# Causal filter and step sizes of a state-space block: half of the filter on TensorE, a shorter series, a comparison on GpSimd, one function table

## The reference, cut to what matters

```
x = lax.conv_general_dilated(x, conv1d_w, (1,), [(DC - 1, 0)], dimension_numbers=('NCH', 'OIH', 'NCH'), feature_group_count=DI)
x = silu(x + conv1d_b[None, :, None])
x_dbl = jnp.einsum('ed,bdl->bel', x_proj_w, x)
dt_lo = x_dbl[:, :DTR]
Bm = x_dbl[:, DTR:DTR + DS]
Cm = x_dbl[:, DTR + DS:]
delta = jnp.einsum('dr,brl->bdl', dt_proj_w, dt_lo)
delta = jax.nn.softplus(delta + dt_proj_b[None, :, None])
...
dBu = jnp.einsum('bdl,bnl,bdl->lbdn', delta, Bm, x)
```

## Time and profile before

| | us |
|---|---|
| median of 3 runs (7186.41 to 7193.9) | 7189.62 |
| the profiled execution, its own time | 7190.81 |
| its span, first to last instruction | 7189.0 |
| block of `filter_and_steps`, first image | 5901.4 to 6027.3 |
| the same, second image | 6417.6 to 6544.0 |

### The profile page before, as it was taken

How to read it: one execution, slowest core, us unless ns; L and a number is a source line. 1 busy time by engine, 2 the same in 40 slices (tenths; PEclk the granted TensorE clock), 3 DMA queues, 4 the chain that set the end, 5 groups by cost and what they waited for, 6 DMA issues and landing times. The chain is left out here.

```text
span 7189.0 us, 96561 instructions
## 1 busy us (share of the span) xinstructions
PE 5186.9 (72%) x22687; PEld 3143.4 (44%) x22687; DVE 5423.3 (75%) x10561; ACT 4492.4 (62%) x11845; POOL 4824.1 (67%) x4571
## 2 busy tenths in 40 slices
PE   7777676776766666666676766676889966757768
PEld 6444444444444344443444443332544434645644
DVE  5777777777777777777777777773769988988972
ACT  4666666666666666666666666775337758958940
POOL 3777777777777777777777777772029965945920
PEclk9999999999999999999999999887999987987989
DMA  7887887878878788787887878886000011231234
GB/s 220 285 250 239 248 250 236 251 238 248 250 237 250 239 248 251 236 251 239 248 251 236 251 238 246 293 284 203 28 21 33 33 49 49 103 110 60 103 122 165
DMA packets 584384, 1400.46 MB, mean 195 GB/s; under 512 B 94035, under 2 KB 258144, under 8 KB 579424
## 3 DMA queue, kind: packets, MB, share of 16 engines
q0 software_dynamic: 308224, 1006.95, 46.3%
q1 hardware_dynamic: 273506, 385.08, 15.8%
q10 hardware_dynamic: 2304, 4.20, 0.2%
HBM read 1314.13 MB, written 81.67 MB: 194 GB/s over the span
## 5 line engine op out<-in xcount | busy, mean ns | idle before, releaser
L627 POOL DMA_INDIRECT st_corners<-corner_table,df_rows x3840 | 3637.9, 947 | 1266.4 <-issue 1048.9
L1000 ACT ACTIVATE st_corners<-st_corners,df_share 128x128 f32<-128x128 f32 x3840 | 1225.7, 390 | 1555.4 <-DMA st_corners<-corner_table,df_rows 1516.0
L900 PE MATMUL df_acc_ps<-df_turned,df_tapw 128*128 128x512 f32 x3840 | 2006.9, 649 | 38.8 <-DMA df_tapw<-in_tap_w_dram 35.4
L889 PE MATMUL df_turn_ps<-main_ident,df_sampled 128*128 128x128 f32 x3840 | 646.6, 295 | 1426.7 <-DVE df_sampled L673 1369.7
L889 PEld LDWEIGHTS df_turn_ps<-main_ident,df_sampled 128*128 128x128 f32 x3840 | 445.5, 148 | 2208.3 <-issue 2096.0
L668 DVE TENSOR_TENSOR st_corners<-st_corners,df_part_ps 128x512 f32<-128x512 f32 x960 | 660.3, 688 | 850.6 <-ACT df_part_ps L1000 838.2
L1000 ACT ACTIVATE df_part_ps<-st_corners,df_share 128x128 f32<-128x128 f32 x3840 | 1178.8, 351 | 35.2 <-DVE df_sampled L673 34.6
L173 PE MATMUL st_conv_ps<-st_ow,st_patch 128*128 128x147 f32 (+1 forms) x6272 | 994.0, 306 | 1.1 <-issue 1.1
L900 PEld LDWEIGHTS df_acc_ps<-df_turned,df_tapw 128*128 128x128 f32 x3840 | 737.5, 210 | 579.5 <-issue 538.7
L173 PEld LDWEIGHTS st_conv_ps<-st_ow,st_patch 128*128 128x128 f32 x6272 | 895.8, 201 | 9.6 <-issue 9.0
L657 DVE TENSOR_TENSOR st_corners<-st_corners,df_weight_ps 128x512 f32<-128x512 f32 x960 | 657.3, 685 | 275.0 <-DMA st_corners<-corner_table,df_rows 270.1
(11 more groups left out here) (373 smaller groups left out, 5613.9 us busy)
## 6 DMA issues: line engine op xcount, KB each, us to landing
df_tapw<-in_tap_w_dram SPq DMA_DIRECT2D x962, 128.0 KB
sc_c_row<-c SPq DMA_DIRECT2D x128, 512.0 KB, 3.6
st_corners<-corner_table,df_rows POOLq DMA_INDIRECT x3840
y_b<-st_outs SPq DMA_DIRECT2D x128, 256.0 KB, 5.2
l1f_w<-in_w_dram SPq DMA_DIRECT2D x32, 1024.0 KB, 6.9
fu_spare<-y_b SPq DMA_DIRECT2D x64, 256.0 KB, 5.4
f_y_in<-y_b SPq DMA_DIRECT2D x64, 256.0 KB, 5.7
u<-dw_u SPq DMA_DIRECT2D x64, 256.0 KB, 2.1
```

The costliest lines, as they stand in the source:

```text
L627: nc.gpsimd.indirect_dma_start(corners[slot][:, j].rearrange("p v c -> p (v c)"), None, tables[g // GPB], bass.IndirectOffsetOnAxis(ap=row ...
L889: t = nc.tensor.transpose(turn_ps[pair][:, j * TILE:(j + 1) * TILE], sampled[pair][:, j, :], ident[:])
L900: m = nc.tensor.matmul(acc_ps[:, h, :], tapw[pair][:, h * P:(h + 1) * P], turned_sb[pair][:], start=first, stop=last, skip_group_check=not ...
L1000: nc.scalar.activation(dst, src, ACT.Copy, scale=share[slot][:, j - VT, v:v + 1]).then_inc(weighed_a, 1)
```

## The change

- Three quarters of the filter of half 0 (chunks 0 to 5, six of the eight) go to TensorE: four products with diagonal weight matrices `diag` per chunk, into PSUM tiles that lie idle at that time. ScalarE builds the four diagonals. VectorE keeps five of the eight units of 1024 columns (`TAPPED`), one after the other and no longer two interleaved.
- The silus follow the new order: silu(0), silu(1), keep_low(0), keep_low(1), soften(0), silu(2), silu(3), soften(1). The loop over c keeps its order on ScalarE, TensorE and VectorE.
- The series runs in a unit in which its leading coefficient is one, so that it needs four operations on each half and not five. The exponential makes e in that unit through its bias, and the logarithm takes it back through its scale.
- The comparison (`large`) moves from VectorE to GpSimd, `bound(c)`. GpSimd runs bound(0), and then for each c: bound(c+1), du(c).
- Two explicit loads name one table that has both exp and log.

```diff
-    SERIES = (1.0 / 5, -1.0 / 4, 1.0 / 3, -1.0 / 2, 1.0)
-    LIMIT = 2.0 ** -5
+    UNIT = 0.2 ** 0.2
+    SERIES = [c / UNIT ** n for n, c in ((4, -1.0 / 4), (3, 1.0 / 3), (2, -1.0 / 2), (1, 1.0))]
+    LIMIT = UNIT * 2.0 ** -5
+    CONVOLVED = (PARTS - 1) * LP // SPAN
+    TAPPED = [(1, 0), (1, 1), (0, PARTS - 1), (1, 2), (1, PARTS - 1)]
...
+        def conv_ps(c):
+            if c in (2, 3):
+                return delta_ps[c - 2][:]
+            return dut_ps[c % 2][:].rearrange("p j d -> p (j d)")
...
+            def convolve(c):
+                pe.wait_ge(u_loaded[c * SPAN // LP], 16 * HALVES)
+                if c >= 4:
+                    pe.wait_ge(active, active_by_pe(c - 4))
+                for k in range(CONV1):
+                    m = nc.tensor.matmul(conv_ps(c), diag[:, k, :], u[0][:, c * SPAN + k:c * SPAN + k + SPAN],
+                                         start=(k == 0), stop=(k == CONV1 - 1))
+                m.then_inc(filtered, 1)
...
+            pe.wait_ge(cleared, HALVES)
+            pe.wait_ge(diagonals, CONV1)
+            for c in range(4):
+                convolve(c)
             project(0)
             widen(0)
             project(1)
+            for c in range(4, CONVOLVED):
+                convolve(c)
+            pe.wait_ge(active, ACTIVE[PARTS - 1])
...
+            for k in range(CONV1):
+                nc.scalar.activation(diag[:, k, :], ident[:], ACT.Copy,
+                                     scale=conv1_sb[:, 0, b, k:k + 1]).then_inc(diagonals, 1)
...
-                    nc.scalar.activation(e_sb[s][h][:], e_sb[s][h][:], ACT.Exp, scale=-1.0).then_inc(exped, 1)
+                    nc.scalar.activation(e_sb[s][h][:], e_sb[s][h][:], ACT.Exp, scale=-1.0,
+                                         bias=log_unit[:]).then_inc(exped, 1)
...
             silu(0)
+            silu(1)
+            nc.scalar.preload_act_table_set("natural_log_exp_and_others")
             keep_low(0)
+            keep_low(1)
             soften(0)
-            keep_low(1)
+            silu(2)
+            silu(3)
+            nc.scalar.preload_act_table_set("natural_log_exp_and_others")
             soften(1)
-            for q in range(1, PARTS):
-                silu(q)
...
+                    if k == 0:
+                        ins = v.tensor_scalar(dst, src, w, None, ALU.mult)
+                    else:
+                        dve.wait_ge(tapped, n * CONV1 + k)
...
-                    own.done(v.tensor_scalar(poly[h][:], e_sb[s][h][:], SERIES[0], SERIES[1], ALU.mult, ALU.add))
-                for term in (0.0, *SERIES[2:]):
+                    own.done(v.scalar_tensor_tensor(out=poly[h][:], in0=e_sb[s][h][:], scalar=SERIES[0],
+                                                    in1=e_sb[s][h][:], op0=ALU.add, op1=ALU.mult))
+                for term in SERIES[1:]:
...
-                for h in both:
-                    v.tensor_scalar(large[h][:], e_sb[s][h][:], LIMIT, None, ALU.is_ge).then_inc(bounded, 1)
...
+            def bound(c):
+                for h in range(HALVES):
+                    pool.wait_ge(exped, HALVES * c + h + 1)
+                    if c >= 1:
+                        pool.wait_ge(stepped, HALVES * (c - 1) + h + 1)
+                    nc.gpsimd.tensor_scalar(large[h][:], e_sb[c % 2][h][:], LIMIT, None, ALU.is_ge).then_inc(bounded, 1)
+
+            bound(0)
             for c in range(GPB):
+                if c + 1 < GPB:
+                    bound(c + 1)
```

More of the change, by code:

```diff
@@ L1 @@
+import math
 from contextlib import ExitStack
@@ L2187, in filter_and_steps @@
         du = [sb(f"du{s}", [P, HALVES, SPAN]) for s in range(2)]
+        diag = sb("diag", [P, CONV1, P])
+        log_unit = sb("log_unit", [P, 1])
         low_ps = pb("low_ps", [P, SPAN])
@@ L2193, in filter_and_steps @@
         cleared = sem("cleared")
+        diagonals = sem("diagonals")
+        filtered = sem("filtered")
         tapped = sem("tapped")
@@ L2214, in cols, with active_by_pe @@
             return slice(c * SPAN, (c + 1) * SPAN)
+        def conv_ps(c):
+            if c in (2, 3):
+                return delta_ps[c - 2][:]
+            return dut_ps[c % 2][:].rearrange("p j d -> p (j d)")
+        ACTIVE = []
+        for q in range(PARTS):
+            ACTIVE.append((ACTIVE[-1] if ACTIVE else 0) + (2 + 1 if q < PARTS - 1 else HALVES))
+        def active_by_pe(c):
+            return c // 2 * 3 + c % 2 + 1
         @block.sync
@@ L2283, in _ @@
         def _(act):
+            for k in range(CONV1):
+                nc.scalar.activation(diag[:, k, :], ident[:], ACT.Copy,
+                                     scale=conv1_sb[:, 0, b, k:k + 1]).then_inc(diagonals, 1)
             act.wait_ge(loaded, 16 * 4)
-            act.wait_ge(one_set, 1)
+            act.wait_ge(one_set, 2)
             def silu(q):
-                for h in range(HALVES):
-                    act.wait_ge(tapped, (q + 1) * CONV1 * HALVES - HALVES + h + 1)
+                if q < PARTS - 1:
+                    for c in range(q * LP // SPAN, (q + 1) * LP // SPAN):
+                        act.wait_ge(filtered, c + 1)
+                        nc.scalar.activation(xs_sb[:, 0, cols(c)], conv_ps(c), ACT.Silu,
+                                             bias=conv_b[:, 0:1]).then_inc(active, 1)
+                for h in (1,) if q < PARTS - 1 else range(HALVES):
+                    act.wait_ge(tapped, CONV1 * (TAPPED.index((h, q)) + 1))
                     part = xs_sb[:, h, q * LP:(q + 1) * LP]
@@ L2312, in soften @@
                     act.wait_ge(valued, 4 * c + 2 * h + 2)
-                    nc.scalar.activation(e_sb[s][h][:], e_sb[s][h][:], ACT.Exp, scale=-1.0).then_inc(exped, 1)
+                    nc.scalar.activation(e_sb[s][h][:], e_sb[s][h][:], ACT.Exp, scale=-1.0,
+                                         bias=log_unit[:]).then_inc(exped, 1)
                 for h in range(HALVES):
                     act.wait_ge(exped, HALVES * c + h + 1)
-                    nc.scalar.activation(ln_sb[s][h][:], e_sb[s][h][:], ACT.Ln, bias=one[:]).then_inc(logged, 1)
+                    nc.scalar.activation(ln_sb[s][h][:], e_sb[s][h][:], ACT.Ln, bias=one[:],
+                                         scale=1.0 / UNIT).then_inc(logged, 1)
             def keep_turned(c):
@@ L2345, in _ @@
             v.memset(one[:], 1.0).then_inc(one_set, 1)
+            v.memset(log_unit[:], math.log(UNIT)).then_inc(one_set, 1)
             for h in both:
@@ L2348, in _, with taps @@
             dve.wait_ge(cleared, HALVES)
-            n = 0
-            for q in range(PARTS):
+            def taps(n):
+                h, q = TAPPED[n]
                 dve.wait_ge(u_loaded[q], 16 * HALVES)
                 for k in range(CONV1):
-                    for h in both:
-                        src = u[h][:, q * LP + k:q * LP + k + LP]
-                        dst = xs_sb[:, h, q * LP:(q + 1) * LP]
-                        w = conv1_sb[:, h, b, k:k + 1]
-                        if k == 0:
-                            ins = v.tensor_scalar(dst, src, w, None, ALU.mult)
-                        else:
-                            dve.wait_ge(tapped, n - HALVES + 1)
-                            ins = v.scalar_tensor_tensor(out=dst, in0=src, scalar=w, in1=dst, op0=ALU.mult, op1=ALU.add)
-                        ins.then_inc(tapped, 1)
-                        n += 1
+                    src = u[h][:, q * LP + k:q * LP + k + LP]
+                    dst = xs_sb[:, h, q * LP:(q + 1) * LP]
+                    w = conv1_sb[:, h, b, k:k + 1]
+                    if k == 0:
+                        ins = v.tensor_scalar(dst, src, w, None, ALU.mult)
+                    else:
+                        dve.wait_ge(tapped, n * CONV1 + k)
+                        ins = v.scalar_tensor_tensor(out=dst, in0=src, scalar=w, in1=dst, op0=ALU.mult, op1=ALU.add)
+                    ins.then_inc(tapped, 1)
+            for n in range(len(TAPPED)):
+                taps(n)
             for c in range(GPB):
```

3 lines of the change are left out of this document (2 added, 1 removed).

## The result

| | before | after |
|---|---|---|
| median, us | 7188.01 (4 runs, 7184.93 to 7193.9) | 7239.69 (4 runs, 7238.44 to 7245.37) |
| ratio, 95% interval | | 1.007 [1.0055, 1.0085] |
| profiled execution, us | 7190.81 | 7238.67 |
| its span, us | 7189.0 | 7236.9 |
| block of image 1, of image 2, us | 126.4, 126.8 | 151.9, 151.8 |

The changed kernel is slower by 51.7 us, outside the range given. The two blocks grew by 25.5 and 25.0 us, and the rest of the span is shorter by 2.6: the whole loss is in the block.

The account below looks back on a forecast made before the run. A circle of waits through ScalarE's order, table loads included, was taken to bound the rounds. Per image 0 - 1.4 + 7.6 - 1.9 = +4.3 us, for two +8.6 on 7190.8, less 1.2: 7199 us, range 7184 to 7222.

Parts of the forecast that it names:

- new circle: Rounds: bound(c+1) waits for next exp, du(c) stands behind it, then turning, keep_low, widening, exp; 11.35 to 12.56 us a round.
- series 2 begins, after the block's start: Head of the block: du(0) starts as before, then 10.86 us instead of 12.27 to series 2, a gain of 1.4.
- five periods: Series 2 to series 7 in each image: 5 x 11.7 = 58.5 us against 50.86, +7.6.
- series 7 to the end of the block: Last chunk and tail: VectorE's work on the last chunk gets 1.9 us shorter, the tail stays as before.
- I take 0.8 us, the middle: Price of one comparison on GpSimd in the rounds, taken between bounds of 0.43 and 1.27 us.
- rival of the port: VectorE's double read of e holds off GpSimd's comparison: 1.3 us in each of six rounds, +7.8 an image, 7214; chance 0.22.
- I take 11.7, because the turning products will mostly follow other PE work closely: Period of the rounds, chosen from 11.35 to 12.56 us, assuming little pause on TensorE before turning.
- du to keep_low: Link of the circle from GpSimd's product through turning to ScalarE's keep_low: 3.85 to 4.52 us.
- keep_low to the series: Link of the circle from keep_low through widening and exp to VectorE's series, without table load: 5.80 to 6.34 us.
- GpSimd or PE dear: Rival: comparisons at 1.27 us, rounds at the lower clock, period 13.5, filter 3 us late; +17 an image, 7224; chance 0.13.
- series 0 starts at 5934.2: Head: after filter, silu(1), keep_low, widening and soften(0), the first series starts at 5934.2 us, before the change 5941.22.
- series 1 starts at 5947.9: Head: silus and table loads ahead of soften(1) leave 2.3 us of the 7 us gain; before the change 5950.25.

Follow-up runs that it names:

- experiment 3: Kernel before with only the comparison moved to GpSimd, bound(c+1) ahead of du(c): 8823.54 us on a chip slow for every kernel, ratio 1.0073.
- experiment 4: Changed kernel with five series operations again, the first reading e once: 8817.76 us on a chip slow for every kernel, ratio 1.0056.
- experiment 8: Changed kernel with GpSimd's comparison cut to 16 of its 512 columns: 7207.43 us, one run.
- Experiment 9: Changed kernel with 16 more transposes a chunk on TensorE ahead of its wait for du, results thrown away: 7229.91 us, ratio 1.0049.
- experiment 1: Changed kernel with du(c) ahead of bound(c+1) in GpSimd's queue: 8761.54 us on a chip slow for every kernel, ratio 0.9982.
- 11: Kernel before with one table for exp and log, and the comparison on GpSimd behind du: 7171.66 us, ratio 0.9971.
- 5: Changed kernel with du(c) ahead of bound(c+1) and five series operations, the first reading e once: 7167.8 us, ratio 0.9971.
- experiment 7: Kernel before with only the filter of six chunks on TensorE and the new order of the silus: 7188.33 us, one run.
- Experiment 10: Version of 5 with soften(1) ahead of the last two silus and TensorE's wait for the silus behind widening and projection: 7176.4 us, ratio 0.9978.
- 2: Changed kernel with the comparison alone back on VectorE: 8764.18 us on a chip slow for every kernel, ratio 0.9984.

## Why the prediction was wrong

The mechanism was right in its structure: the "new circle" of the prediction is the circle in the rows, link by link, no table load is in the loop, keep_low waits for the turning products. The sizes of its links were wrong, all in one direction. The terms per image, predicted and measured:

| term | predicted, us | measured, us | off by |
|---|---|---|---|
| series 2 begins, after the block's start | 59.3 | 63.4 | +4.1 |
| five periods | 5 x 11.7 = 58.5 | 5 x 14.79 = 73.9 | +15.4 |
| series 7 to the end of the block | 14.9 - 1.9 = 13.0 | 14.7 | +1.7 |
| block against before's | +4.3 | +25.5 | +21.2 |

**The step that failed: "I take 0.8 us, the middle".** The comparison on GpSimd costs 1.49 us by itself, median 1488 ns in experiments 3 and 4, beyond my upper bound of 1.27, which was a product of two inputs. One input less did not make it cheaper than that row; I had assumed it must. With the port it was 3.68 us a round instead of 1.7: +1.98, times five +9.9 us. It is the largest single part, and experiment 8 shows its size: with the term cut from 3.68 to 1.48 us its round is 2.2 us shorter. The sentence of the Trainium skill (GPSIMD Engine Reference, Engine selection), by which one-input work is "roughly line-rate", does not hold for this comparison: 1.49 us measured, against the estimate of 0.43 from that page's clock.

**The rival of the port was a part, not a case.** The prediction kept it as an alternative at 1.3 us a round. It came on top, at 0.55 (experiment 4, 3.61 to 3.06; it is in the 1.98 above): the first comparison takes 2.04 us instead of 1.49. The Trainium skill (SBUF — State Buffer, Who interferes with whom) has such a pair exclude each other for whole instructions; the trace agrees that the two hold each other up, and not that it is for the whole instruction here. By the profile's times for the round at 5974.76 the comparison lost 0.55 us, less than one double read (0.70). VectorE's second double read took 1.11 us and ended 0.32 us before that comparison did, so it did not wait for the comparison's end. VectorE pays as well: its predicated copy of two takes 2.11 us beside du for 1.28 in experiment 8, where du is over by then, and its double read 1.71 for 1.30. Those two are off the circle in the rounds and stand on the path in the last chunk: of the predicted gain of 1.9 us they took 1.2. Another 0.4 went between the block's last copy and the scan's memset (0.97 us for 0.60), so that 0.25 was left.

**The clock: "I take 11.7, because the turning products will mostly follow other PE work closely".** They do not. In the circle TensorE waits over 4 us for du each time (4.23 in the round shown, 4.12 to 4.73 in the others from series 2 on), and behind that wait turning takes 1.97 us in every round, widening 3.78. That shows in the circle's two other links: du to keep_low became 4.69 us (bounds 3.85 to 4.52), keep_low to the series 6.42 (5.80 to 6.34): 11.1 instead of the 10.0 that I took, +1.1 a round, +5.5 an image. Experiment 9 shows the cause: with TensorE kept busy both terms fall in the round shown, to 3.81 and 5.50, below my lower bounds, and the mean round by 1.75 us. The prediction treated the clock as a given of the rounds, while the change itself makes the wait that lowers it.

**The rival "GpSimd or PE dear"** had the direction of both, and its upper bounds gave 13.5 us; reality was above in all three terms. The range ended at 7222, just below this rival's 7224, which adds 17 us an image; 25 was the case. (The last step of the sum is off by 0.3 us: 7199.4 less 1.2 is 7198.2. It changes nothing.)

**The head: "series 0 starts at 5934.2", "series 1 starts at 5947.9".** These are 32.8 and 46.5 us into the block; measured 35.8 and 49.1. TensorE's filter products took 16.6 us (16.2 predicted) and began 0.6 us later; together this is 1 us of the delay. Most of the other 2 us is the pair of widening 0 and projection 1, in the timeline of the changed kernel:

```profile
5923.30 1.98 PE L2285 MATMUL ss_delta_ps<-ss_low,ss_dtproj 8*128 8x512 f32 x4 [1.88 <-ACT ss_low L2345]
5925.21 3.60 PE L2265 MATMUL ss_low_ps<-l1i_xs,ss_xproj 128*40 128x512 f32 x4
```

I gave the eight records 3.7 us and they took 5.5; the last four ran at the lower clock, after TensorE had idled 1.88 us just ahead of the first four. That the silus ahead of soften(1) eat the gain was right. The remaining 1.5 us come between series 1 and du(0), where the pair of comparisons stands: 3.2 us (5945.69 to 5948.87) for the 1.7 of the sum. From du(0) to series 2 it was 11.11 us, 10.86 predicted.

**Right as predicted**: that du(c) is held by the wait for exp of chunk c+1. Putting it first took 33 us off the block (experiment 1), and behind the product the comparison on GpSimd even gains: period 8.75 us in 11 against 9.25 with the table alone. The table's worth was stated as 1.41 us in the circle, 1.34 measured. What the filter on TensorE is worth: experiments 5 and 11 have the same ratio with and without it, and 7 by itself shows none.

**Open**: how much the order of the silus and how much TensorE's clock takes in the filter's lost gain. Experiment 10 shows that moving one wait moves the loss, and experiment 7 has a lower clock in rounds of unchanged work. And the ranking of 5 and 11 is not settled, both 0.9971, on different chips.

## What to carry to other kernels

A queue is a chain: before an operation is put on an "idle" engine, ask which later one stands behind it, and what its own wait is for. If that wait is for the next round's data, a loop through all engines closes, and its period is the sum of its links and not the largest engine's time. Here swapping two entries of one queue was worth 33 us a block.

Each stall in such a circle also changes the terms already summed: TensorE, made to wait 4.23 us here, turned at the lower clock, in 1.97 us instead of 1.10. A term's size in the kernel before is measured at the clock before; give both, and take the slower if the change puts a wait ahead of it.

Price an operation that has no row from the nearest one of the same engine upward too: fewer inputs did not mean less time.

## What the runs showed of the hardware

- GpSimd's comparison of 128x512 elements, f32 in and int32 out, takes 1.49 us, more than its product of two f32 inputs at 1.27 us. With 16 columns the pair still took 1.40 us beside VectorE's double read.
- VectorE's operations with two inputs in SBUF and GpSimd's reading ones lengthen each other: comparison 1.49 to 2.04 us, pair of double reads 1.30 to between 1.71 and 3.12 (experiments 1 and 2), predicated copy of two 1.28 to 2.11, product du of two 2.49 to 2.99.
- A dense row of such operations can hold GpSimd off for long: two comparisons that need 3.0 us took 15.91 beside the filter's taps, the first of them 14.34, until the last tap was through. The longest in experiment 3 is 15.62.
- 16 useless transposes a chunk made the blocks 8.9 and 6.2 us shorter; TensorE's granted clock in the rounds was 0.76 with them and 0.56 without.
